# Forward transforms: GpSimd adds the two halves of a piece's squares, TensorE sums half as many columns

## The reference

```python
def _gn(v, G=32, eps=1e-5):
    g = v.reshape(B_, H_, W_, G, C_ // G)
    m = jnp.mean(g, axis=(1, 2, 4), keepdims=True)
    s = jnp.var(g, axis=(1, 2, 4), keepdims=True)
    return ((g - m) / jnp.sqrt(s + eps)).reshape(v.shape)
...
x_ft = jnp.fft.rfft2(xt, s=(M, N)) / scale_fwd      # layer 0: of _gn(x)
a = x_ft[:, :, :nm, :nm]                            # nm = 32
...
x_ft = jnp.fft.fftn(x, axes=(1, 2))[:, :modes, :modes, :]   # layer 2: 16 modes
```

## Time and profile before

| | us |
|---|---|
| median of 3 runs | 17528.62 |
| lowest and highest | 17513.36, 17532.54 |
| the profiled execution's own time | 17533.65 |
| its span, first to last instruction | 17531.2 |
| busy in the span: TensorE (PE) | 11464.3 (65%) |
| VectorE (DVE) | 10577.3 (60%) |
| ScalarE (ACT) | 7828.6 (45%) |
| GpSimd (POOL) | 5522.4 (32%) |
| mean granted TensorE clock | 0.827 of full speed |

### The profile page before, as it was taken

The page is one execution under the profiler, slowest core; times in us unless marked ns, Lnnn a source line. Parts: engine busy times, 40 slices in busy tenths (PEclk is TensorE's granted clock), DMA queues, the critical chain, the costliest instruction groups (busy, mean ns, idle before and its releaser), DMA issues. The chain is left out here.

```text
span 17531.2 us, 298406 instructions
## 1 busy us (share of the span) xinstructions
PE 11464.3 (65%) x106498; PEld 8493.7 (48%) x106498; DVE 10577.3 (60%) x20160; ACT 7828.6 (45%) x13586; POOL 5522.4 (32%) x3307
## 2 busy tenths in 40 slices
PE   8785555999999997999999899756649600000002
PEld 3583333777777776888888788333324300000001
DVE  3115556777777776666666333257736699877773
ACT  5213333666666665555555222624435411444441
POOL 0002333555555553111111354024423399100001
PEclk9757777999999998999999999978879855555555
DMA  6665553111111111010100699855563355100007
GB/s 259 161 131 173 177 186 122 37 38 39 39 36 39 39 39 39 39 58 39 58 39 39 239 364 345 301 190 220 227 250 96 96 202 198 49 11 11 11 11 270
DMA packets 1260011, 2153.75 MB, mean 123 GB/s; under 512 B 95122, under 2 KB 938018, under 8 KB 1168418
## 3 DMA queue, kind: packets, MB, share of 16 engines
q1 hardware_dynamic: 872834, 1631.54, 28.3%
q10 hardware_dynamic: 365344, 446.77, 7.8%
q0 software_dynamic: 20608, 58.22, 1.1%
HBM read 1346.21 MB, written 790.14 MB: 122 GB/s over the span
## 5 line engine op out<-in xcount | busy, mean ns | idle before, releaser
L1005 POOL TENSOR_TENSOR la_s<-la_s,la_mx 128x512 f32<-128x512 f32 x2048 | 2072.0, 1044 | 1799.1 <-DVE la_mx L964 1799.1
L2151 PE MATMUL fp_tp<-fp_idn,fp_f 128*128 128x128 f32 x512 | 89.1, 348 | 3518.3 <-DMA fp_f<-ft 3500.6
L2151 PEld LDWEIGHTS fp_tp<-fp_idn,fp_f 128*128 128x128 f32 x512 | 80.2, 184 | 3527.8 <-issue 3309.7
L956 DVE TENSOR_TENSOR la_s<-la_ps,la_post 128x2048 f32<-128x2048 f32 x512 | 1173.3, 2292 | 907.5 <-PE la_ps L866 907.5
L1042 ACT ACTIVATE la_et<-la_pt 128x512 f32<-128x512 f32 x2048 | 1223.0, 597 | 982.3 <-PE la_pt L879 941.0
L559 PE MATMUL i_fp<-i_v,i_kxm 128*128 128x512 f32 x2048 | 1081.7, 690 | 679.6 <-DVE i_xo L621 416.0
L879 PE MATMUL la_pt<-la_idn,la_s 128*128 128x128 f32 x8192 | 1322.6, 285 | 2.8 <-DVE la_o L979 1.7
L2023 ACT ACTIVATE cs_junk<-cs_num 8x256 f32<-8x256 f32 x1024 | 426.1, 416 | 1865.3 <-DVE cs_num L2086 1630.4
L657 POOL TENSOR_TENSOR i_acc<-i_acc,i_xo 128x4096 f32<-128x4096 f32 x112 | 994.1, 8876 | 719.5 <-DVE i_xo L621 461.5
L964 DVE TENSOR_REDUCE la_mx<-la_s 128x16 f32<-128x1024 f32 x1024 | 1200.8, 1214 | 17.4
L695 ACT ACTIVATE i_sq<-i_xo 128x4096 f32<-128x4096 f32 x128 | 463.0, 3617 | 1479.7 <-DVE i_part L604 688.9
(11 more groups left out here) (245 smaller groups left out, 28633.0 us busy)
## 6 DMA issues: line engine op xcount, KB each, us to landing
f_xt<-in_x SPq DMA_DIRECT2D x128, 1024.0 KB, 8.1
i_xr<-in_x SPq DMA_DIRECT2D x64, 2048.0 KB, 8.3
x<-pj_o SPq DMA_DIRECT2D x64, 2048.0 KB, 10.1
f_xt<-x SPq DMA_DIRECT2D x128, 1024.0 KB, 13.8
i_xr<-x SPq DMA_DIRECT2D x64, 2048.0 KB, 12.0
x<-i_xo ACTq DMA_DIRECT2D x64, 2048.0 KB, 12.7
cs_xt<-x SPq DMA_DIRECT2D x96, 1024.0 KB, 6.8
out<-cs_xt SPq DMA_DIRECT2D x96, 1024.0 KB, 4.8
```

The lines of the kernel that those rows point to most:

```text
L956: nc.vector.tensor_tensor(s[:, S % RS].rearrange("p t h i -> p h t i"), ps[:, :, :, :, :, :].rearrange("p h g e d i -> p h (g e) (d i)"), ...
L1005: nc.gpsimd.tensor_tensor(sv, sv, mb, ALU.subtract).then_inc(s_sub, 1)
```

## The change

GpSimd gets a step per piece: once ScalarE has squared it, it adds the second half of the buffer (row half 1) to the first half in place and signs that on a new semaphore `s_fold`. TensorE's sums wait for `s_fold` in place of `s_sq` and read only the first half: `NR` goes from 2 to 1, in layer 0 and in layer 2 alike. ScalarE's and SyncE's waits stay as they are.

```diff
-    NR = PW // 2048
+    NR = PW // 4096
...
-        s_sq, s_sum = m.sem("sq"), m.sem("sum")
+        s_sq, s_fold, s_sum = m.sem("sq"), m.sem("fold"), m.sem("sum")
...
                 def squares(b, i):
 
-                    pe.wait_ge(s_sq, b * NPC + (XB + 1 + i))
+                    pe.wait_ge(s_fold, b * NPC + (1 + i))
                     if i == 0:
                         pe.wait_ge(s_red, b + 1)
                     for r in range(NR):
...
             def _(pool):
                 pool.sem_inc(s_aofree, 1)
                 with pool.Fori(0, B) as b:
+                    for i in range(NPC):
+                        pool.wait_ge(s_sq, b * NPC + (XB + 1 + i))
+                        half = sq[:, i % 2, 0:PW // 2]
+                        nc.gpsimd.tensor_tensor(half, half, sq[:, i % 2, PW // 2:PW], ALU.add).then_inc(s_fold, 1)
                     pool.wait_ge(s_vs, b * 2 + 2)
                     pool.dma_start(modes[bass.ds(b, 1)].rearrange("a q p n -> p (a q) n"), ao[:, :, :]).then_inc(s_store, 16)
                     pool.wait_ge(s_store, b * 16 + 16)
```

## The result

| | before | changed |
|---|---|---|
| median, us (4 runs each) | 17525.28 | 17755.22 |
| lowest and highest | 17513.36, 17532.54 | 17751.10, 17762.77 |
| the profiled execution's own time | 17533.65 | 17762.77 |
| ratio to before, 95% interval | 1 | 1.0132 (1.012 to 1.0144) |

The change costs 230 us. A loss was forecast, but of 87 us. What the forecast spoke of, the two forward stages, came out near it: 103 us. More than half of the loss lies in a stage that the change does not touch.

The account below looks back on a forecast made before the run. TensorE was taken to bound layer 0's forward stage and loads layer 2's. Terms 38 − 4 (layer 0) + 52 + 1 (layer 2) gave +87 us on the profiled 17533.65, 17620.7; with the median 5 us lower, forecast 17616, range 17570 to 17665.

Parts of the forecast that it names:

- What bounds the stages: Forward stages: TensorE sets layer 0's pace, 5.43 us a piece; loads set layer 2's, 5.42 us.
- The price of an add, 4.5 us: GpSimd, both forward stages: each of 128 adds of 128x2048 within one buffer takes 4.5 us.
- The new loop, 9.4 us a turn: Forward stages: square, add and sums chain over two square buffers; two pieces cost 9.4 us, 4.7 a piece.
- The late first add: GpSimd first waits for its modes' store; first add at T0+16.8 in layer 0, T0+6.9 in layer 2.
- Layer 0, +34 us: Layer 0 forward: images 2 to 8 +5.5 us each, including 3.0 for the clock, +38; image 1 −4.
- Layer 2, +53: Layer 2 forward: images 2 to 8 +7.5 us each, including 1.0 for the clock, +52; image 1 +1.
- The sum: 38 − 4 + 52 + 1: Whole kernel: both forward stages' terms make +87 us on the profiled 17533.65; forecast 17616 us, chance 0.84.
- moved past: GpSimd's store behind 8 adds goes out when it did; SyncE's loads shift into empty queues; both cost nothing.
- the shared port: Rival, forward stages: VectorE's PSUM copies and GpSimd's adds hold each other up, +118 us on top, 17734; chance 0.04.
- The hidden add: Rival, forward stages: adds hide under the 5.43 us pace, TensorE's saving comes through whole, 17459 us; chance 0.04.
- the early store: Rival: layer 0's store lands as soon after issue as layer 2's, adds start 7.0 us earlier, 17554 us; chance 0.05.
- the cheap add: Rival, forward stages: one-buffer adds run like a one-operand copy, 1.8 us each, 17504 us; chance 0.03.

Follow-up runs that it names:

- the run with free store: Kernel before plus adds in layer 0 only, its modes' store in SyncE's queue behind piece 4's load, 32 small matmuls keeping code in place: 17514.11 us, ratio 0.9991.
- the one with tiny adds: Change in layer 0 alone, GpSimd adding only 64 of 2048 columns, store still in GpSimd's queue, 32 small matmuls for code position: 17523.86 us, ratio 0.9992.
- two other kernels: The change in layer 0 alone, 17697.23 us, ratio 1.0099; and the changed kernel with 32 small matmuls behind layer 0's loop, ratio 1.0056.
- +60 twice: Layer 2's stage in the change in layer 2 alone, 17581.76 us, ratio 1.0035, and in the changed kernel with 32 small matmuls, ratio 1.0056.
- its code put back: Changed kernel with 32 small unread matmuls (128 TensorE instructions) run once behind layer 0's forward loop: ratio 1.0056, +95 us against before.
- +128: Kernel before, no adds, with 32 small matmuls behind layer 0's forward loop, moving later TensorE code 128 instructions: ratio 1.0078, +142 us.
- one position: Kernel before, no adds, with 16 small matmuls behind layer 0's forward loop, moving later TensorE code 64 instructions: ratio 1.0122, +211 us.

## Why the prediction was wrong

It said 17616 us (17570 to 17665) and the kernel takes 17755. Step by step:

- **What bounds the stages: right.** TensorE in layer 0, the loads in layer 2; once the store is out of the way, layer 0 gains from shorter sums.
- **The price of an add, 4.5 us: right.** 4.55 measured over 128, 4.48 to 4.59:

```profile
L301 POOL TENSOR_TENSOR f_sq<-f_sq x128: 4482/4550/4592, 17.4 to 11600.4; 128x2048 f32<-128x2048 f32 x128
```

- **The new loop, 9.4 us a turn: right,** 9.45. **The late first add: right,** T0+17.4 and T0+7.3 on the mean for 16.8 and 6.9, with the effect that the run with free store and the one with tiny adds show. In layer 2 the forecast gave the hand-over from the last packet 0.3 us, in layer 0 0.5; neither was enough.
- **Layer 0, +34 us: +39 in the stage** (+36 and +37 in two other kernels). On the mean of images 2 to 8 the last sums end at T0+58.0; 55.2 + 3.0 was summed. Of these 58.0, 0.6 is the later start, which leaves 2.2 for the clock. Before, they end at T0+52.2 on the mean, and the forecast took the 52.7 of one image. So an image costs 5.8 us in place of 5.5. The first image gained 1.7 in place of 4: 7 × 5.8 − 1.7 = 39.
- **Layer 2, +53: +64** (+60 twice). The sum was 7.5 an image. The image looked at above has 8.0, and the mean of images 2 to 8 is 8.7 at the last sums (T0+47.6 against 38.9): some images spend longer at half clock (a granted clock of 0.82 in the second, of 64.0 us). With 0.4 for the later start that leaves 2 us for the clock in place of 1.0. The first image cost 2.7 in place of 1.
- **"The sum: 38 − 4 + 52 + 1": the step that failed.** It held that what the change does to the kernel is what it does in the stage. With its code put back the changed kernel loses 95 us, and its two stages are 36 and 60 us longer, where 87 in all were summed. The rest, 119 us in attention and 13 in the mixing, is the move of TensorE's code by 131 instructions. That the absolute 17613.7 us lies so near the forecast of 17616 is in part luck: the kernel before took 17518.94 on that chip. The part "moved past" asked for queues and stores that are passed and not for code. The trace of before held the sign of it: 215.7 us of waits put down to "issue" at a loop's jump, with the clock at half behind most of them, and a block of code that lands inside each. The jump was the missing term; what another place of it would cost those rows do not say.
- **The rivals.** The total came near that of the shared port (17734), for another reason: VectorE's copies from PSUM take 0.69 us beside adds as before. VectorE was held up by an add in one step only, the one with two tensor inputs in SBUF. The hidden add, the early store and the cheap add did not happen.

## What to carry to other kernels

Where a kernel has long hardware loops, a change in the number of instructions anywhere ahead of a loop can cost more in that loop than the change does in its own place: compare stages, not totals, and time the change a second time with its later code put back in place. Before work is given to an idle engine, read what its queue waits for; an engine that is idle because it waits for its own store is not free, and the store should be moved first. Ask of each small VectorE step beside the new GpSimd work whether it reads two tensors from SBUF.

## What the runs showed of the hardware

- The back jump of attention's loop on TensorE (2108 rows of TensorE a turn) makes it wait 3.4 to 4.2 us a turn, by the place of the code alone, and at one position a second wait of 1.5 us stands within the turn. Every such jump ends 1.3 to 2.0 us, as a rule 1.4, after a 16 KB block of code has landed. The kernel's other loop with a long body (3254 rows, L1120 before) has jumps of 3.3 to 3.9 us too; the three loops of some 800 rows, the forward stages' among them, jump back in 0.2 us.
- The granted clock is down to 0.5 (1.2 GHz) behind all 62 jumps of the changed kernel, with waits of 4.2 us, and behind 50 of the 62 before, with waits of 3.5. That costs more than the longer wait: 72 of 119 us. That positions repeat after 256 instructions rests on two shifts, +128 and −131. Which position is good was found by trying.
- A 64x1 product with two SBUF inputs on VectorE stood 3.93 us beside a GpSimd add of 4.5 us, while copies from PSUM and the one-input form ran at their usual 0.69 and 0.20 us. The Trainium skill (SBUF — State Buffer, Who interferes with whom) says so: a VectorE instruction with two SBUF inputs contends with a GpSimd instruction that reads SBUF, and one with a single input outside the 2-port modes does not. The trace agrees.
- In-place addition of two halves of one buffer costs GpSimd 4.55 us for 128x2048 fp32, as much as one with a second buffer (4.65).

Not tried: adds in layer 2 with an early store. There the first square ends at T0+5.7 and the first add starts at T0+7.3, so at most some 1.6 of the 8.7 us an image lost could come back (an estimate from these two rows).
